# The row tiles of three convolutions: six matmuls of 96 rows, or four of 128 and one of 64

## Time and profile before

| | us |
|---|---|
| median of three runs | 12107.07 |
| the profiled execution | 12072.02 |
| its span, first to last instruction | 12070.2 |
| TensorE matmul busy | 11062.8 (92%) |
| VectorE busy | 7592.0 (63%) |
| GpSimd busy | 5472.2 (45%) |
| ScalarE busy | 3302.3 (27%) |

### The profile page before, as it was taken

The page is one execution under the profiler, slowest core; times in us unless marked ns, Lnnn a source line. Parts: engine busy times, 40 slices in busy tenths (PEclk is TensorE's granted clock), DMA queues, the critical chain, the costliest instruction groups (busy, mean ns, idle before and its releaser), DMA issues. The chain is left out here.

```text
span 12070.2 us, 242619 instructions
## 1 busy us (share of the span) xinstructions
PE 11062.8 (92%) x82492; PEld 10237.2 (85%) x82492; DVE 7592.0 (63%) x19405; ACT 3302.3 (27%) x3654; POOL 5472.2 (45%) x5025
## 2 busy tenths in 40 slices
PE   0999999899989998999899999999879999999999
PEld 0999999666669998998799889987779999999974
DVE  5444444322248886877778777866667676777754
ACT  0222222222222352023322450055622222222210
POOL 0666666333335554555455444544434444444410
PEclk9999999899999999999899999988889999999999
DMA  9666666699976567879765658799845555555569
GB/s 173 136 138 136 137 133 135 133 194 193 192 154 181 136 177 160 183 161 205 159 161 142 167 142 177 164 197 214 197 102 113 104 112 114 107 115 104 116 197 360
DMA packets 1974004, 1907.40 MB, mean 158 GB/s; under 512 B 1224122, under 2 KB 1863968, under 8 KB 1900960
## 3 DMA queue, kind: packets, MB, share of 16 engines
q1 hardware_dynamic: 1973152, 1897.01, 69.9%
HBM read 781.57 MB, written 578.81 MB: 113 GB/s over the span
## 5 line engine op out<-in xcount | busy, mean ns | idle before, releaser
L744 POOL TENSOR_TENSOR rl_wide<-rl_wide,rl_state 96x512 f32<-96x512 f32 x510 | 818.3, 1605 | 812.1 <-ACT rl_state L655 812.1
L273 PE MATMUL du_sum<-du_high,sw_down_high 96*96 96x256 f32 x6132 | 1085.8, 286 | 102.9 <-DVE du_high L335 75.7
L273 PE MATMUL du_sum<-du_low,sw_down_high 96*96 96x256 f32 x6132 | 1118.2, 291 | 0.1
L273 PE MATMUL du_sum<-du_high,sw_down_low 96*96 96x256 f32 x6132 | 1078.2, 284 | 0.0
L940 POOL TENSOR_TENSOR gf_own_low<-gf_sums,gf_own_high 96x2080 fp32r<-96x2080 f32 x128 | 598.5, 4676 | 901.4 <-DVE gf_hid_a L1520 896.4
L1436 PE MATMUL gf_four<-gf_own_high,l_w_hid_high 96*128 96x256 f32 x3072 | 883.8, 288 | 108.4 <-DMA gf_next_low<-gf_own_low 108.4
L273 PEld LDWEIGHTS du_sum<-du_high,sw_down_high 96*96 96x96 f32 x6132 | 831.9, 165 | 111.3 <-DVE du_high L335 78.8
L934 POOL TENSOR_TENSOR gf_sums<-gf_block 96x520 f32<-96x520 f32 x512 | 602.7, 1207 | 666.1 <-DVE gf_hid_a L1520 637.9
L940 POOL TENSOR_TENSOR qk_own_low<-qk_sums,qk_own_high 96x2080 fp32r<-96x2080 f32 x128 | 596.8, 4662 | 666.4 <-ACT qk_own_high L904 666.4
L1436 PE MATMUL gf_four<-gf_next_high,l_w_hid_low 96*128 96x256 f32 x3072 | 874.1, 285 | 0.0
L346 POOL TENSOR_TENSOR du_low<-du_state,du_high 96x128 fp32r<-96x128 f32 x1020 | 613.1, 601 | 573.2 <-DVE du_state L336 573.2
(11 more groups left out here) (214 smaller groups left out, 32209.2 us busy)
## 6 DMA issues: line engine op xcount, KB each, us to landing
qk_next_high<-qk_own_high SPq DMA_DIRECT2D x256, 389.8 KB, 5.2
qk_next_low<-qk_own_low SPq DMA_DIRECT2D x256, 389.8 KB, 5.3
gf_next_high<-gf_own_high SPq DMA_DIRECT2D x256, 389.8 KB, 5.4
gf_next_low<-gf_own_low SPq DMA_DIRECT2D x256, 389.8 KB, 5.5
du_wide<-x SPq DMA_DIRECT2D x32, 3072.0 KB, 17.0
up<-du_wide SPq DMA_DIRECT2D x32, 3072.0 KB, 20.9
rl_wide<-up SPq DMA_DIRECT2D x128, 768.0 KB, 15.8
rl_wide<-x SPq DMA_DIRECT2D x128, 768.0 KB, 16.5
```

Source lines behind the costliest of these rows:

```text
L273: mm = self.nc.tensor.matmul(self.half_line(r, c), w[0:kk, k, :], x[0:kk, (r - 1) % RING, 2 * c:2 * c + 2, k:k + PAIRS], start=(n == 0 and ...
L744: nc.gpsimd.tensor_tensor(at, at, by_sub_block(row), ALU.add).then_inc(placed, 1)
```

## The change

Own and next rows are laid into tiles of 128 and 64 rows. `full` (128 rows) holds the 96 own rows and the first 32 shifted rows. The other 64 shifted rows lie in `left` (128 rows): in its upper half those of high, in its lower half those of low. The weights are laid out alike, `left_twice` holding the high weights of the last 64 rows twice. Then high x high and high x low weights take one matmul of 128 rows each for `full`, low x high weights one of 128 rows, `left` with `left_twice` does high and low together (128 rows), and high `left` with the low weights is a matmul of 64 rows (`LEFT`). Five matmuls make a sum, the third of them with 64 rows.

```
+LEFT = 2 * C2 - 128
-        self.parts = {(w, q): [ph.sb(f"{w}_{q}{k}", [C2, self.rows, PITCH], F32R) for k in range(SLOTS)] ...}
+        self.full = {q: [ph.sb(f"full_{q}{k}", [128, self.rows, PITCH], F32R) ...] for q in ("high", "low")}
+        self.left = [ph.sb(f"left{k}", [128, self.rows, PITCH], F32R) for k in range(SLOTS)]
...
-                sp.dma_start(nxt[0:C, 0:n], own[0:C, 1:n + 1]).then_inc(done[u % SLOTS], 16)
-                sp.dma_start(nxt[C:C2, 1:n + 1], own[C:C2, 0:n]).then_inc(done[u % SLOTS], 16)
+                at = 0 if q == "high" else LEFT
+                sp.dma_start(full[C2:128, 0:n], full[0:128 - C2, 1:n + 1]).then_inc(done[u % SLOTS], 16)
+                sp.dma_start(left[at + C - (128 - C2):at + LEFT, 1:n + 1], full[C:C2, 0:n]).then_inc(...)
+                sp.dma_start(left[at:at + C - (128 - C2), 0:n], full[128 - C2:C, 1:n + 1]).then_inc(...)
...
-    def passes(self, u, w_high, w_low):
-        for q, w in (("high", w_high), ("high", w_low), ("low", w_high)):
-            for ab, n in enumerate(("own", "next")):
-                yield self.parts[n, q][u % SLOTS], w, ab
+    def passes(self, u, full_high, full_low, left_twice, left_low):
+        high, low, left = self.full["high"][u % SLOTS], self.full["low"][u % SLOTS], self.left[u % SLOTS]
+        return ((high, full_high, 128), (high, full_low, 128), (left, left_low, LEFT),
+                (low, full_high, 128), (left, left_twice, 128))
+LOW_FROM = 3
+PASSES = 5
```

The weights are spread by DMA. `kernels_phase` (run twice) and `attention_phase` (once) split them on VectorE into an own part and a shifted part, and SyncE then issues five DMAs and waits for them before the phase ends:

```
+            for d, s in ((full_high[C2:128], shifted["high"][0:top]), (full_low[C2:128], shifted["low"][0:top]),
+                         (left_twice[0:LEFT], shifted["high"][top:C2]), (left_twice[LEFT:128], shifted["high"][top:C2]),
+                         (left_low[0:LEFT], shifted["low"][top:C2])):
+                sp.dma_start(d.bitcast(F32), s.bitcast(F32)).then_inc(spread, 16)
+            sp.wait_ge(spread, 80)
```

More of the change, by code:

```diff
@@ L790, in __init__ @@
         self.sums4 = None if plain else ph.sb("sums4", [C2, self.rows, PITCH])
-        self.parts = {(w, q): [ph.sb(f"{w}_{q}{k}", [C2, self.rows, PITCH], F32R) for k in range(SLOTS)]
-                      for w in ("own", "next") for q in ("high", "low")}
+        self.full = {q: [ph.sb(f"full_{q}{k}", [128, self.rows, PITCH], F32R) for k in range(SLOTS)]
+                     for q in ("high", "low")}
+        self.left = [ph.sb(f"left{k}", [128, self.rows, PITCH], F32R) for k in range(SLOTS)]
         self.zero = ph.sb("zero", [C2, PITCH])
@@ L903, in prepare_high @@
         self.ph.hold(act, self.conved, self.per * (NSTRIP * b + u + 1))
-        self.nc.scalar.copy(self.parts["own", "high"][u % SLOTS][:, :, :], rows).then_inc(self.rounded, 1)
+        self.nc.scalar.copy(self.full["high"][u % SLOTS][0:C2, :, :], rows).then_inc(self.rounded, 1)
     def pool_clear(self, pool):
@@ L939, in pool_batch @@
                 self.ph.hold(pool, quiet, 2 * (NSTRIP * b + u) + 2)
-            g.tensor_tensor(self.parts["own", "low"][u % SLOTS][:, :, :], rows,
-                            self.parts["own", "high"][u % SLOTS][:, :, :], ALU.subtract).then_inc(self.rest, 1)
+            g.tensor_tensor(self.full["low"][u % SLOTS][0:C2, :, :], rows,
+                            self.full["high"][u % SLOTS][0:C2, :, :], ALU.subtract).then_inc(self.rest, 1)
     def wait_conved(self, eng, b, g):
@@ L1052, in _ @@
             dve.wait_ge(combined, 3)
-            v.tensor_copy(high[:, :, :, :], rows4[:, :, :, :]).then_inc(combined, 1)
+            parts = ((rows4[:, 0], full_high[0:C2], full_low[0:C2]), (rows4[:, 1], shifted["high"][:], shifted["low"][:]))
+            for whole, high, _ in parts:
+                last = v.tensor_copy(high, whole)
+            last.then_inc(combined, 1)
             dve.wait_ge(combined, 4)
-            v.tensor_tensor(low[:, :, :, :], rows4[:, :, :, :], high[:, :, :, :], ALU.subtract).then_inc(combined, 1)
+            for whole, high, low in parts:
+                last = v.tensor_tensor(low, whole, high, ALU.subtract)
+            last.then_inc(combined, 1)
         @block.tensor
@@ L1179, in attention_phase @@
         loaded, vec, root, prod, expd = (ph.sem(n) for n in ("loaded", "vec", "root", "prod", "expd"))
+        whole = [ph.sb(f"whole{b}", [C2, len(TILES6), C]) for b in range(B)]
+        full_high, full_low, left_twice, left_low = w_v
+        shifted = {q: ph.sb(f"shifted_{q}", [C2, B, len(TILES6) // 2, C], F32R) for q in ("high", "low")}
+        rounded, rest, spread = ph.sem("rounded"), ph.sem("rest"), ph.sem("spread")
         block = ph.block()
@@ L1187, in _ @@
             sp.dma_start(proj_t[:, :], p["proj_t"]).then_inc(loaded, 16)
+            sp.wait_ge(rest, B)
+            top = 128 - C2
+            for d, s in ((full_high[C2:128], shifted["high"][0:top]), (full_low[C2:128], shifted["low"][0:top]),
+                         (left_twice[0:LEFT], shifted["high"][top:C2]), (left_twice[LEFT:128], shifted["high"][top:C2]),
+                         (left_low[0:LEFT], shifted["low"][top:C2])):
+                sp.dma_start(d.bitcast(F32), s.bitcast(F32)).then_inc(spread, 16)
+            sp.wait_ge(spread, 80)
         @block.vector
@@ L1222, in _ @@
                     ins = nc.vector.tensor_copy(
-                        w_v[:, b, 4 * j:4 * j + 4, :], pk[j][0:C2, 0:4 * C].rearrange("p (t n) -> p t n", t=4))
+                        whole[b][:, 4 * j:4 * j + 4, :], pk[j][0:C2, 0:4 * C].rearrange("p (t n) -> p t n", t=4))
                 ins.then_inc(vec, 1)
+            for b in range(B):
+                dve.wait_ge(vec, NV * (b + 1))
+                nc.vector.tensor_copy(full_high[0:C2, b], whole[b][:, 0:6, :])
+                nc.vector.tensor_copy(shifted["high"][:, b], whole[b][:, 6:12, :]).then_inc(rounded, 1)
+                dve.wait_ge(rounded, b + 1)
+                nc.vector.tensor_tensor(full_low[0:C2, b], whole[b][:, 0:6, :], full_high[0:C2, b], ALU.subtract)
+                nc.vector.tensor_tensor(shifted["low"][:, b], whole[b][:, 6:12, :], shifted["high"][:, b], ALU.subtract)\
+                    .then_inc(rest, 1)
         @block.scalar
@@ L1716, in build @@
         with Phase(nc, "l3") as l3:
-            p["w_hid"] = [l3.sb(f"w_hid_{q}", [C2, 2, 4, 4 * C2], F32R) for q in ("high", "low")]
+            p["w_hid"] = [l3.sb(f"w_hid_{q}", [k, 4, 4 * C2], F32R) for q, k in WEIGHTS]
             kernels_phase(nc, p, ("x1", "x2"))
```

70 lines of the change are left out of this document (38 added, 32 removed).

## The result

The changed kernel takes 13,741.6 us (median of 4 runs, 13,714.1 to 13,756.8) against 12,108.7 (4 runs, 12,071.1 to 12,147.3): a ratio of 1.135, 95% interval 1.131 to 1.139. The profiled execution took 13,714.1 us, its span is 13,712.2.

A forecast was written before the change was run, and what follows sets the result against it. TensorE was taken to bound the gram and gated stages, the raw-row load loop the value stage. 12,072 - 242 - 369 (matmuls) + 737 + 1106 (trips) + 15 (DMAs) + 16 (setup) = 13,335 us, range 12,700 to 13,800.

The forecast's parts named there:

- The bound: TensorE bounds the gram and gated stages; the value stage is bound by its raw-row load loop, 18.41 us a turn.
- The matmuls taken away: One matmul of six fewer per sum: 242 us less in the gram stage, 369 in the gated; value stage hidden.
- 128 rows at the price of 96: In every sum, a 128-row matmul costs what a 96-row one does; at most 0 to 50 us more.
- The trip: Entering and leaving the 64-row form costs 0.36 us a sum: 737 us gram, 1106 us gated, hidden in value.
- one-row trip: In the sweeps, two one-row matmuls amid 96-row ones lose 0.33 us, taken as the guide to the 64-row price.
- The estimate from the Trainium skill: A tiling mode change drains TensorE; two drains of some 166 ns, 0.33 us a sum, would give 13,180 us.
- The clock: Granted clock stays 0.98 in all three stages, nothing added; a rival with falls in the gaps, 600 us, had 0.02.
- DMAs and setup: Six shift DMAs a strip instead of four, hidden in gram and gated stages, +15 us in all; setup +16 us.
- The sum: Whole kernel: the profiled 12,072 us with all terms added gives 13,335 us.
- The first rival: The 64-row matmul costs nothing extra in the sums; 11,517 us including 25 us of stalls; chance 0.14.

The follow-up runs named there:

- rows65: The changed kernel with 65 rows instead of 64 in the third matmul (the added row meets a zero weight): 11,797.0 us, 0.973 of the kernel before.
- pairs: The changed kernel with the 64-row matmul last in even sums and first in odd ones, half as many trips: 12,586.1 us, 1.039 of the kernel before.
- cut64: The kernel before, its own tiles and DMAs, with one of six 96-row matmuls per sum reading only 64 rows: 16,137.7 us, ratio 1.331.
- cut64up: The kernel before, cut as in cut64 except in the first 4 of 32 strips per image, with two gram accumulator banks: 13,822.8 us, ratio 1.143.

## Why the prediction was right, by its own steps

*The bound.* Right. TensorE set the gram and the gated stage. The value stage stayed within 20 us with 18, 15 or 12 matmuls in a group (1181, 1201 and 1164 us); it grew by 19 us where 15 were forecast.

*The matmuls taken away, and 128 rows at the price of 96.* Right: with 65 rows all five stand 0.12 us apart.

*The trip.* The deciding step was right, and somewhat too small: 0.385 us instead of 0.36, 51 us in the gram and 77 in the gated stage. The forecast steps of 0.2, 0.28, 0.2 and 0.12 are 0.21, 0.31, 0.22 and 0.12. That the one-row trip of the earlier trace rows stood for the 64-row one was a guess, and rows65 and pairs show it. The estimate from the Trainium skill ("TensorEngine Tiling (Array Packing)", Key Properties, for the drain, and "TensorE: Matmul & The Clock Gate", Single matmul latency, for its price) had the same cause with 0.33 us; this trace agrees with the drain, and puts it at 0.385.

*The clock.* This is the step that failed. The prediction added nothing, on the ground that the left sweep with its trips every 2.7 us showed no doubled spacing, and gave the clock 0.02 as a rival of 600 us. The granted clock fell from 0.98 to 0.95 in the gram and gated stages, and the longer slow stretches cost about 80 and 106 us, half of what the prediction missed. A trip in each sum is not a trip every 2.7 us. The changed kernel got off lightly, and so the range held by some luck: cut64 shows the same sort of sum staying low for a whole stage, at a cost of some 1900 us, and a twentieth of that would have put the time above the range.

*DMAs and setup.* Hidden, as said, in the changed kernel: the two low shifts into the left tile land 5.9 and 6.1 us after the issue in the gram stage, against 5.3 in the earlier trace rows, and TensorE waited for them 4 us in the gram and 15 us in the gated stage, in 5 of 256 strips. The setup and attention phase grew by 14 us where 16 were forecast.

*The sum.* 13,335 against 13,714 in the profiled execution. Of the 379 us, 128 are the trip's size, some 186 the clock, and 63 the untouched sweeps, which took 5458 us instead of 5395. Every other kernel here took 5432 to 5497 there, whatever it changed, so the profiled execution of before was a quick one. The clock goes with it: by the traces' clock records the sweeps had 731 us at the lower level before, 838 in the changed kernel and 793 to 927 in the others. At half speed 107 us more cost at most 54 of the 63 us; why the lower level came more often there isn't shown.

*The first rival.* "Nothing extra" gave 11,517 us; rows65 is that case, and took 11,797. The rival's 25 us of stalls were too few: 168 us of new idle time of TensorE stand in the two stages. Its room in the gram stage, a strip of 14.3 us that falls to 12.4, isn't what the rows give either (1890/128 = 14.8 us before, 12.8 us of matmuls with 65 rows), but the chain did not fit behind that either.

## What to carry to other kernels

Before cutting a contraction to fit two tiles, look at the form that the profile prints for each matmul (64*128, 65*128): a sum that alternates between forms pays far more than the matmul it saves, and one padding row of zeros can keep it in the large form. If small ones can't be avoided, put them end to end. After removing a bound, add up the chain behind it: here some 320 of the 580 us that were there on paper could be had, since TensorE had been hiding the transfers, and moving one DMA ahead of the others only changed which of them is late.

## What the runs showed that was not expected

- Gaps in each sum cost more after a pause: with six matmuls a sum TensorE ran low for 2 to 6 us after the fold's 2.1 us wait, with the trip in each sum for 7 to 25 us, with a trip for every two sums for 4 to 9; from the stage's start, 6 us without trips, 36 with them, and in cut64 4556.
- The level persists. cut64 and cut64up have the same sums in 28 of 32 strips, at 1.2 GHz in the one and, but for 21 us, at 2.4 GHz in the other. They differ in the entry and in the fold's waits. Since cut64 was low already before its first such wait, the entry is what let the one rise; what the waits alone would do to a stage that had risen in this layout wasn't tried. Why cut64's gram stage stayed low, where its own gated stage rose after 73 us with the same trips, stays open.
- The PEclk column read 1.00 over those 4558 us at the lower pace because the trace has no clock record there. Where the column is to decide something, the spacing of the matmuls is the cross-check.
- The same rows moved within SBUF in two DMAs or three: 581 or 640 ns a packet of 8316 B.
